# Audio tower on one core: the splitting of the 64-expert weights is taken from POOL and given to ACT and DVE inside the attention

## What is computed

```python
h = tok(x, weight, bias)                       # spliced frames, projected
h = h + recurrence(layernorm(h), ...)          # complex linear recurrence
h = h + mixture16(layernorm(h), ...)           # 16 experts, top 2, means by expert
h = h + sparse_attention(layernorm(h), Wq, Wk, Wv, Wo, idx_sample)
h = h + mixture64(layernorm(h), w1, b1, w2, b2, router_w, router_b)   # 64 experts, top 42

# sparse_attention: M = max(Q K_sample) - mean(Q K_sample); the 25 best queries of each head and
# batch attend to all keys, all others get the mean of V; then the product with Wo
# mixture64: h = gelu(x w1[e] + b1[e]); y = h w2[e] + b2[e]; out = sum over e of comb[t, e] y[t, e]
```

## Time and profile before

| | us |
|---|---|
| median of three runs | 2292.79 |
| the profiled execution | 2281.96 |
| its span | 2280.2 |
| sampling, first copy of ACT to its last copy (578.2 to 698.8) | 120.6 |
| `attend`, first instructions to the last on DVE (709.2 to 876.6) | 167.4 |
| n4, to the start of the last mixture (876.8 to 903.7) | 26.9 |

### The profile page before, as it was taken

The page is one execution under the profiler, slowest core; times in us unless marked ns, Lnnn a source line. Parts: engine busy times, 40 slices in busy tenths (PEclk is TensorE's granted clock), DMA queues, the critical chain, the costliest instruction groups (busy, mean ns, idle before and its releaser), DMA issues.

```text
span 2280.2 us, 35396 instructions
## 1 busy us (share of the span) xinstructions
PE 1924.8 (84%) x9464; PEld 1059.3 (46%) x9464; DVE 1802.5 (79%) x2808; ACT 1336.0 (59%) x1966; POOL 1511.6 (66%) x1154
## 2 busy tenths in 40 slices
PE   6789410769996897669999999999999999999998
PEld 4456300446564786434444444444444444444444
DVE  5584700773557874989999999999989999999998
ACT  3000310541342353468888888888878888888887
POOL 2480076005895604348888888888878888888887
PEclk9899655995997898579999999999999999999999
DMA  3521012411332302224444454444454444444443
GB/s 84 154 60 65 1 52 67 82 29 46 107 129 82 104 1 93 86 75 137 137 137 137 137 177 172 139 141 138 138 203 139 142 137 138 144 142 150 151 147 113
DMA packets 122752, 257.24 MB, mean 113 GB/s; under 512 B 40212, under 2 KB 56244, under 8 KB 121012
## 3 DMA queue, kind: packets, MB, share of 16 engines
q1 hardware_dynamic: 119988, 250.78, 34.1%
q0 software_dynamic: 2688, 5.44, 0.7%
HBM read 219.13 MB, written 29.59 MB: 109 GB/s over the span
## 4 chain that ended last, share of the span: by engine, by line
PE 50%; DVE 5%; issue 2%; DMA 1%; POOL 0%; ACT 0%; DVEq 0%; SPq 0%; ACTq 0%; POOLq 0%
PE bank L2160 26%; PE bank L2174 24%; DVE hc L2092 1%; DMA m_share<-expert_shares 1%; DVE hc L2096 1%; DVE bank L2089 1%; DVE m_work L2074 1%; PE bank L2181 0%; DVE m_best L2071 0%; DVE h L2100 0%; DVE m_work L2065 0%; DVE m_ut L780 0%; ACT bank L2012 0%; DVE m_best L2064 0%; PE bank L772 0%
## 5 line engine op out<-in xcount | busy, mean ns | idle before, releaser
L2012 ACT ACTIVATE bank<-bank,m_b 128x896 f32<-128x896 f32 x768 | 752.8, 980 | 196.6 <-PE bank L2160 196.6
L1969 POOL TENSOR_TENSOR hc<-hc 128x896 f16<-128x896 f32 x384 | 724.8, 1888 | 32.0
L2174 PE MATMUL bank<-hc,weights 128*128 128x448 f16 x3072 | 706.9, 353 | 8.3 <-DVE h L2100 7.1
L1967 POOL TENSOR_SCALAR hc<-hc 128x896 f16<-128x896 f32 x384 | 359.8, 937 | 168.4 <-PE bank L2174 129.6
L2092 DVE TENSOR_TENSOR hc<-bank,m_share 128x896 f32<-128x896 f32 x384 | 419.0, 1091 | 48.8 <-ACT bank L2012 5.6
L2160 PE MATMUL bank<-m_u_first,weights 128*128 (+1 forms) x1536 | 421.9, 356 | 24.4 <-DVE hc L2092 11.7
L2174 PEld LDWEIGHTS bank<-hc,weights 128*128 128x128 f16 x3072 | 298.7, 98 | 297.2 <-issue 15.3
L2089 DVE TENSOR_TENSOR bank<-bank,m_share 128x896 f32<-128x896 f32 x384 | 418.6, 1090 | 10.6 <-ACT bank L2012 6.2
L2096 DVE TENSOR_TENSOR hc<-bank,hc 128x896 f16<-128x896 f32 x384 | 415.3, 1082 | 5.4 <-ACT hc L2015 5.4
L2160 PE MATMUL bank<-m_u_second,weights 128*128 (+1 forms) x1536 | 417.7, 354 | 0.0
L2015 ACT ACTIVATE hc<-bank 128x896 f16<-128x896 f32 x384 | 352.0, 917 | 38.6 <-DVE bank L2089 26.0
(11 more groups left out here) (320 smaller groups left out, 2300.4 us busy)
## 6 DMA issues: line engine op xcount, KB each, us to landing
m_share<-expert_shares SPq DMA_DIRECT2D x384, 448.0 KB, 3.5
ew_raw<-e_w_dram SPq DMA_DIRECT2D x32, 512.0 KB, 4.5
expert_factors<-ew_made SPq DMA_DIRECT2D x24, 512.0 KB, 3.1
weights<-expert_factors SPq DMA_DIRECT2D x12, 1024.0 KB, 9.2
expert_slots<-lru_zeros SPq DMA_DIRECT2D x1, 7296.0 KB, 28.6
lru_wst<-w_dram SPq DMA_DIRECT2D x16, 256.0 KB, 2.7
weights<-w_dram SPq DMA_DIRECT2D x1, 4096.0 KB, 12.1
xs<-x_dram SPq DMA_DIRECT2D x4, 996.0 KB, 12.7
```

The source lines that it names most:

```text
L1967: g.tensor_scalar(h_first[:, x, 1], hs[:, x], 1.0 - SHARE, 1.0, ALU.mult, ALU.mult).then_inc(first_of[1], 1)
L1969: g.tensor_tensor(h_second[:, x, 1], hs[:, x], h_first[:, x, 1], ALU.subtract).then_inc(second_of[1], 1)
L2012: sc.activation(bank, bank, ACT.Gelu, bias=b1[:, bass.ds(grp * GE + e, 1), c]).then_inc(gelu[c], 1)
L2174: last = t.matmul(banks_y[:, q], k.weights[:, grp % 2, 2 + m, at], hh[:, e % 2, c, q * HW:(q + 1) * HW], start=(grp > 0 and e == 0 and c = ...
```

## The change

No piece is split by POOL any more, and none in the norms n3 and n4. Pieces 0 to 15 are split in the sampling, one a chunk, pieces 16 to 31 in `attend`, one for two batches. The split is three instructions. ACT rounds (`act_first`, L1771) and multiplies the raw piece by 64 into one of two new buffers `wide` (`act_wide`, L1776), and DVE adds first * (1 - 64) to it (`dve_second`, L1784). In the sampling `act_first(c)` stands in ACT's `work(c)` behind quarter 1 and `act_wide(c)` behind quarter 3; `dve_second(c - 1)` stands in DVE's `work(c)` behind quarter 1, and that of piece 15 behind the loop. In `attend` ACT has `act_first` at the end of even steps and `act_wide` at the end of odd steps, and DVE `dve_second` at the end of even steps, for the piece of the pair before. The load of piece n now waits for `widened` of piece n - 2. SP's list keeps its form, and the wait for the last stores stands at the end of `attend`. The loops of ACT and DVE in these two blocks, and POOL's pairs, are written out or looped anew for this; PE's loops stay.

```diff
 class ExpertWeights:
-        self.left = sb("left", [128, PIECE])
+        self.wide = sb("wide", [128, 2, PIECE])
...
     def sync_load(self, sp, n):
         if n >= 2:
-            sp.wait_ge(self.raw_read, n - 1)
+            sp.wait_ge(self.widened, n - 1)
...
-    def pool_pieces(self, pool, first, end):
-        g = self.nc.gpsimd
-        for n in range(first, end):
-            raw, left, out = self.raw[:, n % 2, :], self.left[:], self.place(n)
-            pool.wait_ge(self.raw_in[n % 2], 16 * (n // 2 + 1))
-            if n - 2 >= GROUP:
-                pool.wait_ge(self.k.kept_out[n % 2], 16 * ((n - GROUP) // 2))
-            g.tensor_copy(out[:, 0], raw).then_inc(self.rounded, 1)
-            pool.wait_ge(self.rounded, n + 1)
-            if n:
-                pool.wait_ge(self.split, n)
-            g.tensor_tensor(left, raw, out[:, 0], ALU.subtract).then_inc(self.raw_read, 1)
-            pool.wait_ge(self.raw_read, n + 1)
-            g.tensor_scalar(left, left, 1.0 / SHARE, 1.0, ALU.mult, ALU.mult).then_inc(self.widened, 1)
-            pool.wait_ge(self.widened, n + 1)
-            g.tensor_tensor(out[:, 1], left, out[:, 0], ALU.add).then_inc(self.split, 1)
+    def act_first(self, act, n):
+        act.wait_ge(self.raw_in[n % 2], 16 * (n // 2 + 1))
+        if n - 2 >= GROUP:
+            act.wait_ge(self.k.kept_out[n % 2], 16 * ((n - GROUP) // 2))
+        self.nc.scalar.activation(self.place(n)[:, 0], self.raw[:, n % 2, :], ACT.Copy).then_inc(self.rounded, 1)
+
+    def act_wide(self, act, n):
+        if n >= 2:
+            act.wait_ge(self.split, n - 1)
+        self.nc.scalar.activation(self.wide[:, n % 2], self.raw[:, n % 2, :], ACT.Copy, scale=1.0 / SHARE).then_inc(self.widened, 1)
+
+    def dve_second(self, dve, n):
+        out = self.place(n)
+        dve.wait_ge(self.rounded, n + 1)
+        dve.wait_ge(self.widened, n + 1)
+        self.nc.vector.scalar_tensor_tensor(out[:, 1], out[:, 0], 1.0 - 1.0 / SHARE, self.wide[:, n % 2], ALU.mult,
+                                            ALU.add).then_inc(self.split, 1)
...
 sampling, ACT
+                        if q == 1:
+                            k.expert_weights.act_first(act, c)
+                    k.expert_weights.act_wide(act, c)
...
 sampling, DVE
+                        if q == 1 and c:
+                            k.expert_weights.dve_second(dve, c - 1)
...
+                k.expert_weights.dve_second(dve, NC - 1)
...
 attend, ACT
+                if b % 2 == 0:
+                    k.expert_weights.act_first(act, NC + b // 2)
+                else:
+                    k.expert_weights.act_wide(act, NC + b // 2)
...
 attend, DVE
+                if b % 2 == 0 and 2 <= b <= B:
+                    k.expert_weights.dve_second(dve, NC + b // 2 - 1)
```

More of the change, by code:

```diff
@@ L351, with norm_statistics @@
 DEEP, AHEAD = 4, 3
-def norm_statistics(nc, k, name, table, pieces=None, width=CH, tile=HALF, count=NC):
+def norm_statistics(nc, k, name, table, width=CH, tile=HALF, count=NC):
     tiles = count * (width // tile)
@@ L368, in norm_statistics @@
         v = k.bank[0:tile, DEEP, 0:tiles]
-        if pieces:
-            @block.sync
-            def _(sp):
-                k.expert_weights.sync_pieces(sp, *pieces)
-            @block.gpsimd
-            def _(pool):
-                k.expert_weights.pool_pieces(pool, *pieces)
         def span(c):
@@ L1176, in _ @@
                        allow_small_or_imprecise_dtypes=True).then_inc(made, 1)
-                first, end = PIECES_SAMPLE
-                for c in range(NC):
-                    norm.pool_diagonal(pool, c, c % 2)
-                    if 1 <= c <= end - first:
-                        k.expert_weights.pool_pieces(pool, first + c - 1, first + c)
+                with pool.Fori(0, NC // 2) as i:
+                    for j in range(2):
+                        norm.pool_diagonal(pool, 2 * i + j, j)
                 g.memset(expand[:], 0.0).then_inc(made, 1)
@@ L1207, in work @@
                         last.then_inc(kx_copied, 1)
-                chunks(act, work)
+                        if q == 1:
+                            k.expert_weights.act_first(act, c)
+                    k.expert_weights.act_wide(act, c)
+                for c in range(NC):
+                    work(c, c % 2)
                 act.wait_ge(step_pe, 1)
@@ L1266, in _ @@
                 link(v.memset(cand[:], SENT))
-                chunks(dve, work)
+                for c in range(NC):
+                    work(c, c % 2)
+                k.expert_weights.dve_second(dve, NC - 1)
                 dve.wait_ge(step_pe, 1)
@@ L1462, in _ @@
                                 pattern=[[NU, NH], [0, DH]], channel_multiplier=-1).then_inc(made, 1)
-            k.expert_weights.pool_pieces(pool, *PIECES_ATTEND)
         @block.scalar
@@ L1503, in step @@
                 output_copy(b - 2, x - 2)
-            batches(act, step)
+                if b % 2 == 0:
+                    k.expert_weights.act_first(act, NC + b // 2)
+                else:
+                    k.expert_weights.act_wide(act, NC + b // 2)
+            for b in range(B):
+                step(b, b)
             exponentials(B - 1, B - 1)
@@ L1588, in step @@
                 residual(b - 3, x - 3)
-            batches(dve, step)
-            for b in range(B, B + 3):
+                if b % 2 == 0 and 2 <= b <= B:
+                    k.expert_weights.dve_second(dve, NC + b // 2 - 1)
+            for b in range(B + 3):
                 step(b, b)
@@ L1711 @@
 GROUP = 2 * PIECES
-PIECES_N3, PIECES_SAMPLE, PIECES_ATTEND, PIECES_N4 = (0, 5), (5, 19), (19, 29), (29, NG * GROUP)
+PIECES_SAMPLE, PIECES_ATTEND = (0, NC), (NC, NG * GROUP)
 class ExpertWeights:
@@ L1730, in __init__ @@
         self.rounded = k.semaphore("ew_rounded")
-        self.raw_read = k.semaphore("ew_raw_read")
         self.widened = k.semaphore("ew_widened")
@@ L2259, in audio_tower @@
             nc.all_engine_barrier()
-        norm_statistics(nc, k, "n2", 4, None, CW, TW, NCW)
+        norm_statistics(nc, k, "n2", 4, CW, TW, NCW)
         first_mixture(nc, k)
@@ L2263, in audio_tower @@
             k.expert_weights = ExpertWeights(nc, k, inner)
-            norm_statistics(nc, k, "n3", 5, PIECES_N3)
+            norm_statistics(nc, k, "n3", 5)
             sparse_attention(nc, k)
-            norm_statistics(nc, k, "n4", 6, PIECES_N4, CW, TW, NCW)
+            norm_statistics(nc, k, "n4", 6, CW, TW, NCW)
         second_mixture(nc, k, out)
```

## The result

The changed kernel takes 2328.57 us (median of four runs, 2320.03 to 2329.89). The kernel before, run beside it, has a median of 2286.26 (four runs, 2275.74 to 2297.51). The ratio is 1.0176, 95% interval 1.0115 to 1.0238: slower by over 1%, as forecast, and 2333 was forecast. The profiled execution took 2327.77 us, its span 2326.0 against 2280.2.

The account below looks back on a forecast made before the run. PE was taken to bound the sampling, and the round trip attend's batches without pieces. The sum 0.5 + 0.7 + 40 + 15 - 4 - 6 = +46 us on a base of 2287 gave 2333 us, range 2303 to 2362.

Parts of the forecast that it names:

- The new wait: Sampling: ACT's rounding waits for a load behind a store needing dve_second; 6.7 us for each of six pieces, +40 us.
- T + 8.4: Sampling: T is the end of DVE's quarter 1; PE's samples start at T + 8.3 to 8.4, undisturbed at T + 1.7.
- The clock: Sampling: PE's clock goes to half in each of six waits, costing 2.5 us each (range 0 to 4.6), +15 us.
- The instructions themselves in the sampling: Sampling: first chunk costs 0.5 us, the dve_second behind the loop 0.7 us, other iterations without a wait 0.
- attend: attend: silent POOL shortens batches, the new instructions add 1.25 us a pair; 4.73 us a batch, -4 us in all.
- n4: n4: without pieces DVE ends earlier and no store is waited for, so the mixture starts earlier, -6 us.
- n3: n3: PE was busy all the time and DVE's last steps came after the last piece, 0 us.
- The clock stays up: Rival, sampling: the wait is there but the clock stays up or returns at once; +31 us, 2318; chance 0.17.
- The wait is longer: Rival, sampling: the load takes 6.1 us and the clock is low all through; about +69, 2356; chance 0.14.
- attend gets slower too: Rival, attend: DVE's 1.2 and ACT's 2 x 1.0 us all lie on the round trip; +26, 2363; chance 0.06.
- No wait: Rival, sampling: nothing waits if dve_second comes a whole iteration earlier; -9 us, up to -29, 2258 to 2278; chance 0.08.
- The rule of the Trainium skill: DVE and GpSimd lock their shared ports exclusively; by that alone attend would gain 24 us.

Follow-up runs that it names:

- Experiment 1: Changed kernel with DVE making the second part of piece c in its work(c), one chunk earlier: 2267.06 us, ratio 0.9914 to the kernel before.
- experiment 3: Changed kernel with PE's sampling loop written out and six unread 512-column products filling PE's gap in iterations 10 to 15: 2303.94 us.
- the control: Changed kernel with only PE's loop of the sampling written out, no products added: 2336.49 us.
- the kernel with all three cut: Experiment 1's kernel with all three instructions of a piece cut to 8 of 1024 columns in attend: 2250.48 us.
- experiment 7: Changed kernel, but POOL splits 19 pieces before attend, ACT and DVE 13 in attend, DVE in halves, load ahead of store: 2256.63 us, ratio 0.9868 to before.
- Experiment 2: Changed kernel with POOL splitting pieces 0 to 15 (2 in n3, 14 in sampling), ACT and DVE only attend's 16: 2267.24 us, ratio 0.9910 to before.

## Why the prediction was right, step by step

- **The new wait, +40 us: right in place and cause, and 3 us too large.** It was told from the order of two instructions: `act_first(n + 2)` comes in the iteration in which the store of piece n is only released. The trace has six long waits of ACT, the first of 6.82 us, and PE resumes at T + 8.4. Experiment 1, which moves only that, gives back 59.5 us. PE's own wait was 6.3 rather than 6.7 us the first time; at full clock experiment 3 leaves 6.2 an interval, so 37 us.
- **The clock, +15 us: right in mechanism, a little too small.** Filling the gap gave back 15.2 us, but from the control. In the changed kernel PE is busy 59.57 us where the control has 56.07, so an estimate for it is 15.2 + 3.5 = 18.7. The clock stayed low for 6.8 us after the first resumption instead of 4.7; the one wait that lasted longer did not cost more clock.
- **What was missed, +3.6 us.** I took 1.2 us for every second part and wrote that POOL no longer disturbed DVE. POOL has one long instruction left in the stage (4.14 us), and one second part fell into it. The step that failed was to count POOL's piece instructions as all that it does. 37 + 18.7 + 3.6 is 59.3, and 59.5 were measured.
- **The instructions themselves in the sampling, +1.2 us: at the upper end** of the -0.3 to +1.2 measured (experiment 1); these executions don't tell it from nothing.
- **attend, -9.4 in place of -4: mechanism right, base too long.** The costs on the round trip were forecast as 0.8 and 0.45 us and measured as 0.75 and 0.43. But I added them to 4.11 us, the batch of the kernel before, and the batch of the new code without pieces is 3.99. 31 x 0.12 makes 3.7 us. The maxima of DVE wait for PE's scores 0.40 us before and 0.22 to 0.29 in the kernel with all three cut. Why the base is shorter was not tried. ACT's and DVE's loops are written out in the change, and that fits: the version of experiment 7 has them written out too and 3.99 us in its last batches, which have no piece, and the one step of the kernel before that stands behind its loop took 3.99 as well.
- **n4, -5.5 in place of -6, n3 0: right.** Experiment 2 keeps two pieces on POOL in n3 and has no loss there (23.4 us against 23.6 in experiment 1, which has none).
- **The rivals.** "The clock stays up" is refuted by PEclk; the filled kernel of experiment 3, at 2303.94 us, is what it would have looked like (I had put it at 2318). "The wait is longer" is true of one wait in six. "attend gets slower too" fell, since the delays of the two engines don't add up. "No wait" would have been right with the second part one chunk earlier.
- The rule of the Trainium skill (SBUF — State Buffer, Who interferes with whom), an exclusive lock of the ports shared by DVE and GpSimd, taken by itself, spoke for a faster kernel. It held in `attend` (2.54 to 0.62 us), and the sampling outweighed it. It held once more where I did not look for it: 4.81 us against 1.22.

## What to carry to other kernels

When a chain of load, split and store goes through two engines that run a loop iteration apart, write down for each buffer which iteration frees it and which wants it again; here a slack of one iteration (7.25 us) hid the whole way of 6.2 us, and none exposed it in every pass, with the clock of TensorE on top. Moving a DMA ahead in its queue helps only down to the next dependency through the same instruction, so look for the buffer behind the buffer. And count all that an engine still does in a stage, not only what is taken from it: one instruction of 4 us at the wrong moment is enough.

## What the runs showed of the hardware

**DVE and POOL, who comes first.** In the changed kernel POOL's selection had run for 0.37 us when the second part came, and DVE's took 4.81 us and POOL's its usual 4.14. In the control of experiment 3 DVE came 0.51 us ahead:

```profile
702.29 1.23 DVE L1785 SCALAR_TENSOR_TENSOR ew_made<-ew_made,ew_wide 128x1024 f16<-128x1024 f16 x1
```

```profile
702.80 4.71 POOL L1174 TENSOR_SCALAR_AFFINE_SELECT at_expand<-at_expand 128x3200 bf16<-128x3200 bf16 x1 [0.16 <-POOL at_expand L1171]
```

DVE took its 1.23 and POOL 0.57 us more. So in both orders the one that had begun kept its usual time, and the other paid. DVE's short instructions that read a bank, beside POOL's memset and selection in the changed kernel, were not slower (0.47 us at 688.41 and at 689.62). In the kernel before, DVE's one-hot products L1534 are not the only ones that POOL's pieces slow. The scaling L1564, a tensor by one value a partition, both from SBUF, takes 1.55 us for two beside POOL and 0.52 later, with POOL silent. The prediction named L1534 alone for the long batches of 6.54 us.

```profile
745.15 1.55 DVE L1564 TENSOR_SCALAR att_prob<-att_prob,att_tot 100x166 f32<-100x166 f32 x2
```

```profile
801.18 0.52 DVE L1564 TENSOR_SCALAR att_prob<-att_prob,att_tot 100x166 f32<-100x166 f32 x2
```

**The clock of a stage can differ between executions of equal work.** n3 is the same on PE in all kernels. Windows of the kernel before and of experiment 1, 533 to 556 us:

```profile
533.00:556.00 23.00, 23.00 (x95) 17.49 (x95) 5.56 (x12) 5.75 (x12) 20.48 (x14) 0.50 0.33 104
```

```profile
533.00:556.00 23.00, 20.73 (x160) 16.44 (x159) 9.62 (x22) 8.96 (x19) 0.00 (x0) 0.87 0.00 1
```

With PE never idle the clock stayed at half all through, and n3 took 39.3 us; where it had come up, n3 took 23.6. It came up with pieces on POOL (experiment 2) and without (experiment 1), and stayed low with (before) and without (after). The part up to n3 has two lengths as well, 531 to 535 and 547 us. In the last version, which has the long one, the first 100 us have a clock of 0.74, and 0.91 in the kernel before, which has the short one. Each is some 16 us, and the times of one and the same kernel lie in groups so far apart (experiment 1: 2251 to 2258 and 2267 to 2270). What decides it was not tried.
